# Two graph-attention layers on 32 pairs of graphs: another order of layer 1's products, a timetable of its own for the last pair, and the first weights in order of use

## The reference

```
# layer 0
h = relu(layernorm(x));  q, k, v = h@Wq + bq, h@Wk + bk, h@Wv + bv     # 8 heads of 64
x = x + softmax(q k^T / 8 + (adj == 0 ? -1e9 : 0)) v
# layer 1
h = relu(layernorm(x));  q, k, v = h@Wq'^T, h@Wk'^T, h@Wv'^T
rel = adj^T * (q k^T);  rel = rel / norm(rel, axis=2)
x = x + rel v
```

## Time and profile before

| | us |
|---|---|
| median of 3 runs (2464.73 to 2466.9) | 2466.06 |
| the profiled execution | 2466.99 |
| its span, first to last instruction | 2465.2 |
| TensorE busy in it | 2396.9 (97%) |
| ScalarE busy | 1682.6 (68%) |
| VectorE busy | 1411.2 (57%) |
| GpSimd busy | 1296.1 (53%) |

### The profile page before, as it was taken

How to read it: one execution, slowest core, us unless ns; L and a number is a source line. 1 busy time by engine, 2 the same in 40 slices (tenths; PEclk the granted TensorE clock), 3 DMA queues, 4 the chain that set the end, 5 groups by cost and what they waited for, 6 DMA issues and landing times.

```text
span 2465.2 us, 53413 instructions
## 1 busy us (share of the span) xinstructions
PE 2396.9 (97%) x19252; PEld 1304.5 (53%) x19252; DVE 1411.2 (57%) x4432; ACT 1682.6 (68%) x4108; POOL 1296.1 (53%) x1159
## 2 busy tenths in 40 slices
PE   5899999999999999999999999999999999999986
PEld 2455555555555555555555555555555555555543
DVE  4555665555665555665555666555666555665543
ACT  4676766677766776766767766777766776766762
POOL 2555555555555555555555555555555555555541
PEclk9999999999999999999999999999999999999998
DMA  6566665775666666765666765666666666665642
GB/s 179 121 125 129 150 134 126 136 142 129 147 137 124 135 146 126 149 136 120 139 138 133 146 140 120 140 139 132 150 138 119 140 141 130 151 134 119 125 112 64
DMA packets 938792, 329.13 MB, mean 134 GB/s; under 512 B 885920, under 2 KB 886176, under 8 KB 938528
## 3 DMA queue, kind: packets, MB, share of 16 engines
q1 hardware_dynamic: 936272, 323.35, 63.1%
q10 hardware_dynamic: 2256, 2.36, 0.4%
HBM read 73.93 MB, written 33.55 MB: 44 GB/s over the span
## 4 chain that ended last, share of the span: by engine, by line
PE 89%; DMA 4%; ACT 3%; POOL 1%; DVE 1%; issue 1%; SPq 1%; DVEq 0%; ACTq 0%; POOLq 0%
PE B L677 75%; PE O L677 7%; PE S L751 7%; DMA probs_t<-halves 2%; DMA h0t<-h_halves 1%; ACT h L414 1%; ACT probs L474 1%; POOL h_halves L361 1%; PE B L707 1%; ACT h_halves L421 1%; POOL halves L375 1%; SPq L319 0%; POOL guess L356 0%; DMA h1t<-h_halves 0%; DVE masked L611 0%
## 5 line engine op out<-in xcount | busy, mean ns | idle before, releaser
L375 POOL TENSOR_TENSOR halves<-probs,halves 128x512 f16<-128x512 f32 x512 | 593.2, 1163 | 573.5 <-ACT halves L482 573.4
L474 ACT ACTIVATE probs<-masked,neg_max 128x256 f32<-128x256 f32 x1024 | 508.0, 497 | 229.6 <-DVE neg_max L611 229.5
L611 DVE CUSTOM_DVE_ANT_0 masked<-S,mask 128x256 f32<-128x256 f32 x1024 | 384.6, 418 | 126.4 <-PE S L751 126.3
L677 PE MATMUL B<-h0t,wq 128*128 128x512 f16 x1536 | 356.4, 382 | 32.2 <-DMA h0t<-h_halves 31.5
L361 POOL TENSOR_TENSOR h_halves<-h,h_halves 128x512 f16<-128x512 f32 x256 | 295.4, 1160 | 164.2 <-ACT h_halves L421 164.0
L677 PE MATMUL B<-wvt,h1t 128*128 128x512 f16 x1536 | 349.6, 381 | 9.8 <-DMA h1t<-h_halves 9.8
L677 PE MATMUL B<-h0t,wk 128*128 128x512 f16 x1536 | 352.8, 379 | 0.0
L677 PE MATMUL B<-wv,h0t 128*128 128x512 f16 x1536 | 352.2, 379 | 0.0
L677 PE MATMUL B<-h1t,wm 128*128 128x512 f16 x1536 | 346.9, 379 | 0.0
L482 ACT ACTIVATE halves<-probs 128x512 f16<-128x512 f32 x512 | 322.5, 630 | 16.2
L677 PEld LDWEIGHTS O<-v,probs_t 128*128 128x128 f16 x6144 | 248.3, 98 | 130.2 <-DMA probs_t<-halves 11.5
(11 more groups left out here) (70 smaller groups left out, 2894.7 us busy)
## 6 DMA issues: line engine op xcount, KB each, us to landing
x_in<-in_x_dram SPq DMA_DIRECT2D x128, 256.0 KB, 3.4
x_res<-in_x_dram SPq DMA_DIRECT2D x128, 256.0 KB, 3.7
out_dram<-result SPq DMA_DIRECT2D x128, 256.0 KB, 2.5
probs_t<-halves SPq DMA_TRANSPOSE x512, 2.8
h0t<-h_halves SPq DMA_TRANSPOSE x128, 3.2
h1t<-h_halves SPq DMA_TRANSPOSE x128, 3.3
rv<-in_L_gnn_Wq_dram SPq DMA_DIRECT2D x1, 1024.0 KB, 8.3
rq<-in_L_gnn_Wk_dram ACTq DMA_DIRECT2D x1, 1024.0 KB, 5.3
```

The costliest lines, as they stand in the source:

```text
L375: nc.gpsimd.tensor_tensor(halves[:, n % RING, 1, :], probs[:, n % 2, :, :].rearrange("p t n -> p (t n)"), halves[:, n % RING, 0, :], ALU.s ...
L474: ins = nc.scalar.activation(probs[:, n % 2, i, :], masked[:, n % 2, i, :], ACT.Exp, bias=neg_max[:, n % 2, i:i + 1], scale=-1.0, accum_ou ...
L611: ins = nc.vector.tensor_tensor_reduce(out=masked[:, n % 2, i, :], in0=S[n % 4][:, i, :], in1=mask[:, i, :], scale=SCORE, scalar=BIG, op0= ...
L677: ins = nc.tensor.matmul(dst, left(i), right(j), start=(n == 0), stop=(n == len(pairs) - 1))
```

## The change

**A new table.** `SLOTS`, `BESIDE` and `LOADS` are replaced by `PRODUCT_AT`, `LAYER0` and `LAYER1`, which give each step of a pair its slot counted from that pair's start, and `timetable` and `in_order` sort the steps of all pairs by slot and by a place inside it. The period stays 26.

**Layer 1.** Before: rv 0 to 3, rq 0 to 3, rel 0, rel 1, out 0 to 3. After: rq 0 to 3, rv 0, rel 0, rel 1, rv 1, rv 2, rv 3, out 0 to 3. rq 0 waits for all four tiles of h1t, rv for none. The scale of layer 1's layer norm is in slot 37 (before: 38), the square sums and scales of rel 4 to 6 slots sooner.

**Layer 0.** v 0 is the first product and waits for its own tile only; q 0 follows and waits for all. scores 0 goes from slot 5 to 6 and the masks, exps and pv steps of the first head pair go with it by one slot. v 2, q 3 and k 1 are one or two slots sooner.

**The last pair.** It has its own timetable (`LAST_...`): q 3 and k 3 are at 14.5 and 15.5, scores 2 and 3 at 17 and 21 (usual: 19 and 26), the masks and pv steps up to five slots sooner, residual and layer norm two.

**The first weights.** Wv, Wq and Wk of layer 0 are loaded in this order in two halves each by ScalarE's queue, which waits for the second x tile first; their high and low halves are made in two parts each.

```diff
+    PERIOD = 26
+    PRODUCT_AT = {("v", 0): 0, ("q", 0): 1, ("k", 0): 3, ("v", 1): 4, ("v", 2): 5, ("v", 3): 7, ("q", 1): 9,
+                  ("k", 1): 10, ("q", 2): 13, ("k", 2): 14, ("q", 3): 15, ("k", 3): 24,
+                  ("rq", 0): 42, ("rq", 1): 43, ("rq", 2): 44, ("rq", 3): 45, ("rv", 0): 46, ("rel", 0): 47,
+                  ("rel", 1): 48, ("rv", 1): 49, ("rv", 2): 51, ("rv", 3): 54,
+                  ("out", 0): 58, ("out", 1): 60, ("out", 2): 63, ("out", 3): 64}
+    PROJECT = [(kind, n) for kind, n in PRODUCT_AT if kind in ("q", "k", "v")]
+    RELATE = [(kind, n) for kind, n in PRODUCT_AT if kind in ("rv", "rq", "rel", "out")]
+
+
+    SCORED = [6, 13, 19, 26]
+    MASKED = [6, 9, 13, 16, 19, 22, 26, 28]
+    MULTIPLIED = [10, 11, 13, 14, 17, 18, 20, 21, 23, 24, 26, 27, 29, 30, 31, 32]
+
+    LAST_PRODUCT_AT = {**PRODUCT_AT, ("q", 3): 14.5, ("k", 3): 15.5}
+    LAST_SCORED = [6, 13, 17, 21]
+    LAST_MASKED = [6, 9, 13, 15, 17, 19, 21, 23]
+    LAST_MULTIPLIED = [10, 11, 13, 14, 17, 18, 19, 20, 21, 22, 23, 24, 25, 26, 27, 28]
+    LAYER0 = {"x_in": [-25, -25, -24, -24], "ln0_stats": [-14, -14, -13, -13], "ln0_power": [-13],
+              "ln0_scale": [-10], "ln0_apply": [-8, -8, -5, -2], "ln0_split": [-8, -8, -5, -2],
+              "x_res": [13, 13, 14, 14], "residual": [17, 23, 28, 34]}
+    LAYER1 = {"ln1_stats": [35, 35, 36, 36], "ln1_power": [36], "ln1_scale": [37], "ln1_apply": [38] * TILES,
+              "ln1_split": [38] * TILES, "squares": [49, 50], "rel_scale": [50, 51], "rel_split": [51, 52]}
+
+    def timetable(product_at, score_at, mask_at, multiply_at, sooner):
+
+        tensor = [(slot, 0, "scores", m) for m, slot in enumerate(score_at)]
+        tensor += [(slot, 1, kind, n) for (kind, n), slot in product_at.items()]
+        tensor += [(slot, 2, "pv", n) for n, slot in enumerate(multiply_at)]
+        others = [(slot + 1, 0, "norm", m) for m, slot in enumerate(multiply_at[3::4])]
+        others += [(slot + 1, 1 if kind == "v" else 3, kind, n) for (kind, n), slot in product_at.items()]
+        others += [(slot + 2, 5, "inverse", m) for m, slot in enumerate(mask_at[1::2])]
+        for j, slot in enumerate(mask_at):
+            others += [(slot, 2, "mask", 2 * j), (slot, 4, "mask", 2 * j + 1)]
+            others += [(slot + e, 7, kind, 2 * j + e) for e in range(2) for kind in ("exp", "split")]
+        for layer in (LAYER0, LAYER1):
+            for n in range(TILES):
+                others += [(at[n] - (sooner if 20 < at[n] < 45 else 0), 8 if kind[0] == "x" else 6, kind, n) for kind, at in layer.items() if n < len(at)]
+        return tensor, others
+
+    def in_order(steps):
+
+        order = []
+        for p in range(-1, PAIRS):
+            for i, (slot, place, kind, n) in enumerate(steps[p == PAIRS - 1]):
+                if p >= 0 and not (p == 0 and slot < 0):
+                    order.append((PERIOD * p + slot, place, p, i, kind, n))
+                elif p < 0 and (kind, n) in SETUP:
+                    order.append((PERIOD * p + slot, place, p, i, "setup_" + kind, n))
+        return [(kind, n, p) for _, _, p, _, kind, n in sorted(order)]
+
     HALVED = [st for st in RELATE if st[0] in ("rq", "rv")]
     NPC, NRC, NRH = len(PROJECT), len(RELATE), len(HALVED)
-    REL_LAST = RELATE.index(("rel", 1)) + 1
+    H1_LAST = max(RELATE.index(("rel", 1)), RELATE.index(("rv", TILES - 1))) + 1
 
     SETUP = [st for st in RELATE if st[0] in ("rq", "rv") or st == ("rel", 0)]
     NSETUP = len(SETUP)
 
...
+    USUAL = timetable(PRODUCT_AT, SCORED, MASKED, MULTIPLIED, 0)
+    LAST = timetable(LAST_PRODUCT_AT, LAST_SCORED, LAST_MASKED, LAST_MULTIPLIED, 2)
+    TENSOR_PLAN, PLAN = [in_order(steps) for steps in zip(USUAL, LAST)]
     KINDS = ("q", "k", "v", "rv", "rq", "rel", "out", "setup_rv", "setup_rq", "setup_rel")
-    PRODUCTS = [step for step in pairs(TENSOR_PLAN) if step[0] in KINDS]
+    PRODUCTS = [step for step in TENSOR_PLAN if step[0] in KINDS]
...
-            sp.dma_start(stage[0], wq0.rearrange("(t p) n -> p t n", p=P)).then_inc(w_loaded[0], 16)
             sp.dma_start(adj_in, adj.rearrange("(t p) n -> p t n", p=P)).then_inc(adj_loaded, 16)
             for n in range(TILES):
                 turn_h(0, n, 0)
             for n, w in enumerate((wv1, wq1, wk1)):
 
-                sp.wait_ge(w_low, n + 1)
-                sp.dma_start(stage[n], w.rearrange("(t p) n -> p t n", p=P)).then_inc(w_loaded[3 + n], 16)
-
-            for kind, n, p in pairs(PLAN):
+                sp.wait_ge(w_low, 2 * n + 2)
+                sp.dma_start(stage[n], w.rearrange("(t p) n -> p t n", p=P)).then_inc(w_loaded[n], 16)
+
+            for kind, n, p in PLAN:
...
-                        sp.wait_ge(r_product, NRC * (p - 1) + REL_LAST)
+                        sp.wait_ge(r_product, NRC * (p - 1) + H1_LAST)
...
+            act.wait_ge(x_loaded[1], 16)
+            for n, w in enumerate((wv0, wq0, wk0)):
+                rows = w.rearrange("(t p) n -> p t n", p=P)
+                for part in range(2):
+                    ts = slice(2 * part, 2 * part + 2)
+                    act.dma_start(stage[n][:, ts, :], rows[:, ts, :]).then_inc(w_part[n][part], 16)
...
             def weight_high(n, w, scale):
-                act.wait_ge(w_loaded[n], 16)
-                nc.scalar.activation(w[:, 0, :, :], stage[n], ACT.Copy, scale=scale).then_inc(w_high, 1)
+                for part in range(2):
+                    ts = slice(2 * part, 2 * part + 2)
+                    act.wait_ge(w_part[n][part], 16)
+                    nc.scalar.activation(w[:, 0, ts, :], stage[n][:, ts, :], ACT.Copy, scale=scale).then_inc(w_high, 1)
 
             for n in range(2):
                 ln_apply(0, x_in, n, 0, h_low[0], 0)
             for n in range(2):
                 h_high_half(0, n, 0, h_turned[0][n], 0)
-            act.dma_start(stage[1], wk0.rearrange("(t p) n -> p t n", p=P)).then_inc(w_loaded[1], 16)
-            weight_high(0, wq, QS)
+            weight_high(0, wv, WS)
             for n in range(2, 4):
                 ln_apply(0, x_in, n, 0, h_low[0], 0)
             for n in range(2, 4):
                 h_high_half(0, n, 0, h_turned[0][n], 0)
-            act.dma_start(stage[2], wv0.rearrange("(t p) n -> p t n", p=P)).then_inc(w_loaded[2], 16)
-            weight_high(1, wk, WS)
-            weight_high(2, wv, WS)
+            weight_high(1, wq, QS)
+            weight_high(2, wk, WS)
...
-            for n, (w, scale) in enumerate(((wq, QS), (wk, WS), (wv, WS))):
-                dve.wait_ge(w_high, n + 1)
-                nc.vector.scalar_tensor_tensor(w[:, 1, :, :].rearrange("p t n -> p (t n)"),
-                                               stage[n].rearrange("p t n -> p (t n)"), scale,
-                                               w[:, 0, :, :].rearrange("p t n -> p (t n)"),
-                                               ALU.mult, ALU.subtract).then_inc(w_low, 1)
+            for n, (w, scale) in enumerate(((wv, WS), (wq, QS), (wk, WS))):
+                for part in range(2):
+                    ts = slice(2 * part, 2 * part + 2)
+                    dve.wait_ge(w_high, 2 * n + part + 1)
+                    nc.vector.scalar_tensor_tensor(w[:, 1, ts, :].rearrange("p t n -> p (t n)"),
+                                                   stage[n][:, ts, :].rearrange("p t n -> p (t n)"), scale,
+                                                   w[:, 0, ts, :].rearrange("p t n -> p (t n)"),
+                                                   ALU.mult, ALU.subtract).then_inc(w_low, 1)
...
+                    if p == 0 and n == 0:
+                        pe.wait_ge(w_low, 2 * ("v", "q", "k").index(kind) + 2)
                     if kind == "v":
-                        if p == 0 and n == 0:
-                            pe.wait_ge(w_low, 3)
+                        pe.wait_ge(h_turned[0][n], 16 * (p + 1))
                         ins = product(dst[:, :], lambda i: h0t[:, p % 2, i[0], i[1], col(n)],
                                       lambda j: wv[:, j[0], j[1], :], over_features)
                     else:
-                        if p == 0 and n == 0:
-                            pe.wait_ge(w_low, 1 if kind == "q" else 2)
-                        if (kind, n) == PROJECT[0]:
+                        if (kind, n) == ("q", 0):
                             for t in range(TILES):
                                 pe.wait_ge(h_turned[0][t], 16 * (p + 1))
...
                     if kind == "rq":
+                        if n == 0:
+                            for t in range(TILES):
+                                pe.wait_ge(h_turned[1][t], 16 * (p + 1))
                         ins = product(dst[:, :], lambda i: wm[:, i[0], i[1], col(n)],
                                       lambda j: h1t[:, j[0], j[1], :], over_features)
                     elif kind == "rv":
-                        pe.wait_ge(h_turned[1][n], 16 * (p + 1))
```

(39 more changed lines are left out.)

23 lines of the change are left out of this document (5 added, 18 removed), and 10 rows, old and new, of tables (BESIDE, SLOTS).

## The result

The changed kernel takes 2499.16 us (2496.12 to 2499.42) where the kernel before takes 2465.39 us on the same chip: ratio 1.0138, interval [1.0126, 1.015]. The prediction was 2461.0 with a range up to 2476. The page of the changed kernel, to be read beside the earlier trace rows: the span, the busy time of the engines, and the group of rq's matmuls with the idle time before it.

What follows compares the result with a forecast made beforehand. TensorE, busy in 97% of the span, was taken to bound the kernel. Start -7.7, middle +16 and end -12.5 give -4.2, rounded to -5: span 2465.2 to 2460.2, median 2461.0 us, range 2443 to 2476.

Steps and rivals of the forecast that it cites:

- The middle: 29 turns between first and last pairs: 15.4 us new waits, plus 6, minus 5.3 old waits; +16 us, between -5 and +35.
- VectorE scale from 11.68, h1 from 12.67: Layer 1's layer norm, us after a pair's last pv: scale starts at 11.68, ScalarE's h1 at 12.67, 0.97 sooner.
- Late landings: Transposed h1t tiles landing late in middle turns, each delay now a wait before rq0: 6 us, from 0 to 10.
- The middle eats all: Rival: rq0's wait for the fourth h1t tile decides from 0.88 us a turn; at 1.3, 2477 us; chance 0.17.
- The bound of the middle, +35: Upper bound for the 29 turns: 1.0 us wait per turn if SyncE's out2 store and unit 3's transposes slow h1's.
- The start: Up to the first pairs: Wv loaded first, v0 at 18 to 20 us; -7.7 us, between -5 and -10.
- nine issues of 0.5 us, done near 9.8, so they delay nothing: ScalarE's weight load issues at the start end before the layer norm's scale at 11.9, costing 0 us.
- the wait of scores 1: Scores 1 waits for k1's evacuation: 1.2 us in pair 0, 2.7 in pair 1.
- the rule on shared DMA engines: Early weights slow the last two x tiles by about 1 us; the start gains 6.7 instead of 7.7.
- The end: Last pair: sooner scores 3, rv0 covering rel0's wait; idle and clock losses 31 to 19 us; -12.5, bounds -8 and -15.

Runs made afterwards that it cites:

- the first experiment: Changed kernel with GpSimd's layer 1 layer norm power moved from slot 36 to 36.5, after unit 3's low half: 2465.53 us, ratio 1.0006 to the kernel before.
- the run with two low halves: Changed kernel with the layer 1 power moved from slot 36 to 34.9, so two GpSimd low halves follow it: 2559.71 us, ratio 1.0387 to the kernel before.

## Why the prediction was wrong

**The middle, the step that failed: "VectorE scale from 11.68, h1 from 12.67".** The start of the scale was right and its length was not: 1.94 us instead of 0.99, because its first instruction was held. The prediction took the length of the scale from a turn of before, where k1's low half on VectorE made it start late, at e+12.65, and GpSimd's low half was past. Moving a chain of small instructions 0.97 us forward moved it beside another engine's instruction, and that neighbour was not looked up. In numbers for the 29 turns: a usual wait before rq0 is 1.53 us, 44.4 in all, where 15.4 were predicted. The surplus of 1.0 a turn, 29.0 in all, is the hold, which the first experiment takes away again (-0.94 a turn).

Late landings were rightly sized: all 29 waits come to 50.2 us, so 5.8 lie above the usual wait, and 6 were predicted. Missing was what a long wait does to TensorE. Stretches of the changed kernel and its timeline there:

```profile
732.50:735.30 2.80, 0.50 (x3) 0.01 (x1) 1.93 (x6) 2.27 (x5) 1.75 (x2) 1.00 1.09 246
735.30:739.60 4.30, 4.21 (x12) 1.59 (x13) 3.31 (x14) 1.72 (x5) 1.17 (x1) 0.60 0.97 244
...
735.39 7.03 PE L663 MATMUL B<-h1t,wm 128*128 128x512 f16 x24 [2.39 <-DMA h1t<-h_halves]
```

After an idle 2.39 us rq0 ran at 0.60 of the clock, between its two levels of 1.2 and 2.4 GHz over the 4.3 us, and rq0 and rq1 took 7.03 us instead of 5.34. It happened twice in the 29 turns, 3.4 us. 50.2 + 3.4 - 5.3 is 48.3, and 47.6 was measured.

The rivals stood on the right wait. *The middle eats all* named it, rq0 for the fourth h1t tile, and its point of decision: 0.88 us a turn. The wait was 1.73 a turn, beyond its 1.3. The bound of the middle, +35, allowed 1.0 us a turn for it, taken from contention of SyncE's queue, a cause that did not come: the transposes were issued at e+16.42 and landed in 3.3 us at the median as before. The range was too narrow at the top because the scale was given no bound of its own. It was also narrower than the bounds of its three terms, which add up to 35 - 5 - 8 = +22, or 2488; the measured time lies above this too, since the middle alone passed its bound.

**The start was right in kind and 3.3 us too good.** First matmul at 18.58 (18 to 20), pair 0's last pv at 104.6 (103.7, from 111.1 before): -6.5 where -7.4 was worked out. One term was missing and one too small. First, "nine issues of 0.5 us, done near 9.8, so they delay nothing": they ended at 10.44, and ScalarE's table load of 1.28 us, which ran at 2.34 before, ahead of everything, now stands behind them; h came at 11.78 though shift was done at 10.0. Second, the wait of scores 1 in pair 0's turn came in its place, but at 3.40 us where 1.2 was predicted: k1's product ended at 78.8, but its high half started on ScalarE only at 81.67, behind one unit's exps, a high half of wvt and a tile of h. After the wait the clock fell:

```profile
79.80:83.20 3.40, 0.02 (x2) 0.02 (x4) 1.55 (x3) 2.99 (x6) 3.19 (x3) 1.00 0.43 96
83.20:86.50 3.30, 3.30 (x28) 1.74 (x29) 2.07 (x9) 1.42 (x5) 0.00 (x0) 0.65 0.75 150
...
83.18 1.83 PE L736 MATMUL S<-k_st,q_st 64*128 64x256 f16 x24 [3.40 <-DVE k_st L582]
...
84.94 4.05 PE L663 MATMUL B<-wv,h0t 128*128 128x512 f16 x12
```

v0 took 4.05 us instead of 2.75. In pair 1 scores 1 waited 2.58 (2.7). Then pair 1's turn brought the middle's hold, 2.66 us of wait and 1.68 of half clock. The early weights did not hold up x: shift was done sooner than before, at 10.0 against 11.9, so the microsecond that the rule on shared DMA engines would have taken did not show. That it was not there is not shown either, since Wq's load, which followed x at once in the kernel before, is gone from that place.

**The end was right**, 118.5 us against the 117.4 that -12.5 gives, and nearly so in each step. TensorE's timeline, against the earlier trace rows:

```profile
2434.35 1.22 PE L663 MATMUL O<-v,probs_t 128*128 128x64 f16 x36 [1.47 <-DVE attn L611]
...
2457.56 13.32 PE L663 MATMUL B<-h1t,wm 128*128 128x512 f16 x48 [11.99 <-DMA h1t<-h_halves]
...
2488.36 5.34 PE L663 MATMUL B<-rv,rel_t 128*128 128x512 f16 x24 [1.87 <-DVE rv L620]
```

Idle before rq0 was 12.0 us (12.4), rq0's start at the low clock cost 2.5 (2.3), out0 waited 1.9 (2.2). One wait came in another place: a pv behind rv2 waited 1.5 us for attn, where 0.4 was given to pv 15.

## What to carry to other kernels

When a chain of small instructions is moved in time, read what the engines next to it do at its new place, instruction by instruction, and price each small VectorE instruction with two SBUF inputs, and TENSOR_SCALAR with one, at up to the length of the GpSimd instruction beside it. Cure it by order: let GpSimd do its long instruction while the chain still waits for something else, rather than cutting it. Before a product that needs all tiles of a landing, put one that needs only the first.

## What the runs showed of the hardware

The hold was to be seen in the kernel before, had its rows been read by maximum and not by median. Duration of the shift, the last of the small layer norm instructions, there (min/median/max in ns, the start in us):

```profile
L557 DVE SCALAR_TENSOR_TENSOR shift<-moments,rstd x64: 161/164/1057, 11.7 to 2413.1; 128x4 f32<-128x4 f32 x64
```

It struck 31 of the 64 there, in layer 0's layer norm of the next pair (e+27.19 in a usual turn), where it could be seen off the path. And instructions with a single SBUF input are held too. The first row is the kernel before's, where 29 instances of var started under a low half of h and took 0.65 to 0.67 us, until its end; the second is the changed kernel's, where one instance was held, as in the kernel with the later power:

```profile
L548 DVE TENSOR_SCALAR var<-moments x64: 170/171/672, 9.6 to 2411.0; 128x4 f32<-128x4 f32 x64
...
L514 DVE TENSOR_SCALAR ln_work<-ln_work x64: 169/170/1124, 9.4 to 2446.5; 128x4 f32<-128x4 f32 x64
```

So two inputs are not the condition by themselves. No run here shows in which performance mode these instructions ran.

What reads PSUM is not held: of the 1024 mask instructions of the kernel before, 490 overlap a long GpSimd instruction, and none takes over 0.43 us. In the turn shown above k1's low half takes its 0.74 us although GpSimd's power starts inside it, and the pair of statistics, with one large SBUF input, takes 1.28 beside a low half. At the start, though, VectorE's weight halves, two SBUF inputs, took 3.06 us for the two of Wv and for those of Wq while GpSimd worked on h, and 2.34 for Wk's after it.

TensorE's clock fell after some waits and not after others of the same length: in the changed kernel after 2.66, 2.55 and 2.30 us, but not after 2.75 and 2.33 (all between the products). What tells them apart is open; a border at 2.4, as the expectation of the run with two low halves had it, does not fit these rows. Once it has fallen, a product of 12 matmuls takes 1.68 us longer, which is more than many of the waits that bring it about: in the run with two low halves the clock cost 29 us more than in the changed kernel and the longer waits 25.6.
